# A decoder layer's cross-attention: the chunk of a key piece stands between its transposes and its weighting, not behind the weighting

## The reference

```python
qh = split_heads(layernorm(x) @ Wq)      # 8 heads of 128
kh = split_heads(context @ Wk)
vh = split_heads(context @ Wv)
sim = einsum('hid,hjd->hij', qh, kh) * 128 ** -0.5
mean = mean(sim, axis=-1, keepdims=True)
sim = (sim - mean) * 1.5 + mean
attn = softmax(sim, axis=-1)
out = einsum('hij,hjd->hid', attn, vh)   # heads side by side, then
x = x + out @ Wout + bout
```

## Time and profile before

| | us |
| --- | --- |
| median of 3 runs (2559.46 to 2560.4) | 2560.4 |
| profiled execution, its own time | 2556.83 |
| its span, first to last instruction | 2555.0 |
| PE busy | 2504.5 |
| DVE busy | 1912.5 |
| ACT busy | 1611.2 |
| granted clock of TensorE, mean over the span | 0.999 |

### The profile page before, as it was taken

The page is one execution under the profiler, slowest core; times in us unless marked ns, Lnnn a source line. Parts: engine busy times, 40 slices in busy tenths (PEclk is TensorE's granted clock), DMA queues, the critical chain, the costliest instruction groups (busy, mean ns, idle before and its releaser), DMA issues. The chain is left out here.

```text
span 2555.0 us, 47085 instructions
## 1 busy us (share of the span) xinstructions
PE 2504.5 (98%) x17639; PEld 2284.5 (89%) x17639; DVE 1912.5 (75%) x3606; ACT 1611.2 (63%) x3049; POOL 157.9 (6%) x208
## 2 busy tenths in 40 slices
PE   7999989999999999999999999999999999999998
PEld 6899868999999999989999899999999999999987
DVE  5899777777777777768777777777777777777787
ACT  6899646565656566565666566656655666655666
POOL 1344220000000000000000000000000000000013
PEclk9999999999999999999999999999999999999999
DMA  7655441002100210012000300031002100110001
GB/s 218 194 160 148 149 174 33 17 17 90 43 24 19 79 54 18 16 67 75 17 17 21 112 18 17 17 108 34 17 17 83 50 17 17 66 69 18 29 1 34
DMA packets 61326, 151.68 MB, mean 59 GB/s; under 512 B 11456, under 2 KB 25024, under 8 KB 61152
## 3 DMA queue, kind: packets, MB, share of 16 engines
q1 hardware_dynamic: 55504, 136.02, 16.4%
q0 software_dynamic: 3248, 12.72, 1.5%
q10 hardware_dynamic: 2400, 0.59, 0.1%
HBM read 126.10 MB, written 23.20 MB: 58 GB/s over the span
## 5 line engine op out<-in xcount | busy, mean ns | idle before, releaser
L1733 PE MATMUL xo_ps<-pt_hi,values 128*128 128x256 f32 x4096 | 950.3, 298 | 2.4 <-DVE pt_lo L1836 2.3
L1755 ACT CAST pt_hi<-xt_ps 128x512 fp32r<-128x512 f32 x1024 | 593.6, 585 | 550.4 <-PE xt_ps L1722 531.7
L1836 DVE TENSOR_TENSOR pt_lo<-xt_ps,pt_hi 128x512 fp32r<-128x512 f32 x1024 | 704.4, 688 | 235.3 <-ACT pt_hi L1755 230.3
L1824 DVE TENSOR_SCALAR_CACHE_REDUCE xprobs<-xs_ps 128x1024 f32<-128x1024 f32 x512 | 627.0, 1225 | 178.1 <-PE xs_ps L1657 173.2
L1733 PEld LDWEIGHTS xo_ps<-pt_hi,values 128*128 128x128 f32 x4096 | 693.0, 188 | 6.1 <-DVE pt_lo L1836 2.6
L1722 PE MATMUL xt_ps<-ident,xprobs 128*128 128x128 f32 x4096 | 603.4, 272 | 0.0
L1762 ACT ACTIVATE xprobs<-xprobs,xneg_max 128x1024 f32<-128x1024 f32 x512 | 591.4, 1155 | 0.2 <-DVE xneg_max L1831 0.2
L1733 PE MATMUL xo_ps<-pt_lo,values 128*128 128x256 f32 x2048 | 570.1, 278 | 0.0
L1722 PEld LDWEIGHTS xt_ps<-ident,xprobs 128*128 128x128 f32 x4096 | 487.6, 140 | 62.1
L1733 PEld LDWEIGHTS xo_ps<-pt_lo,values 128*128 128x128 f32 x2048 | 388.3, 190 | 2.3
L1657 PE MATMUL xs_ps<-k_hi,q_hi 128*128 128x512 f32 x1024 | 327.3, 400 | 1.2 <-DVE values L1884 0.9
(11 more groups left out here) (235 smaller groups left out, 2510.2 us busy)
## 6 DMA issues: line engine op xcount, KB each, us to landing
v_split<-ctx_split SPq DMA_DIRECT2D x68, 768.0 KB, 5.7
xq<-x_split SPq DMA_DIRECT2D x64, 512.0 KB, 3.3
values<-rel_split SPq DMA_DIRECT2D x32, 256.0 KB, 3.5
ctx_split<-ctx_out POOLq DMA_DIRECT2D x8, 768.0 KB, 4.0
q_split<-attn_late SPq DMA_DIRECT2D x16, 256.0 KB, 2.9
k_split<-attn_late SPq DMA_DIRECT2D x16, 256.0 KB, 3.7
values<-q_split SPq DMA_DIRECT2D x32, 128.0 KB, 3.6
values<-k_split SPq DMA_DIRECT2D x32, 128.0 KB, 3.9
```

Of the source, the lines that this page charges most:

```text
L1733: last = pe.matmul(o_ps[:, 0:GQ], v[:, vs], pt[:, c % 3, GQ * j:GQ * (j + 1)], start=c == 0 and j == 0 and m == 0, stop=c == PIECES - 1 an ...
L1755: act.copy(pt_hi[:, c % 3, :], t_ps[:, c % 3, :]).then_inc(t_rounded, 1)
L1824: dve.tensor_scalar(probs[:, par if kind == "A" else 1 - par, t, CHUNK * i:CHUNK * (i + 1)], s_ps[:, buf, :], LOGIT, None, ALU.mult, ALU.m ...
L1836: dve.tensor_tensor(pt_lo[:, c % 3, :], t_ps[:, c % 3, :], pt_hi[:, c % 3, :].bitcast(F32), ALU.subtract).then_inc(t_ready, 1)
```

## The change

`with_pieces` gets a switch, `weigh_first`. With the switch off, as it is unless it is given, the items of piece c now stand between the transposes of c and the weighting of c-2. With the switch on they stand where they were, behind the weighting. It is on for `STEP_8` and `LAST_8`. Since pieces 0 and 1 have no weighting behind their transposes, nothing moves there. In an ordinary step nine chunks change places with a weighting: those at pieces 2, 4, 6, 7, 8, 10, 12, 14 and 15. DVE's, ACT's and SP's lists stay as they are, since they have no item `"W"`.

```diff
-def with_pieces(extra, ahead=()):
+def with_pieces(extra, ahead=(), weigh_first=False):
 
     items = list(ahead)
     for c in range(PIECES):
         items.append(("T", c))
+        if not weigh_first:
+            items += extra.get(c, [])
         if c >= 2:
             items.append(("W", c - 2))
-        items += extra.get(c, [])
+        if weigh_first:
+            items += extra.get(c, [])
     return items + [("W", PIECES - 2), ("W", PIECES - 1)]
...
 STEP_8 = with_pieces({0: [("K+", 2)], 1: [("I",), ("K+", 3)], 2: [("Q+",), ("out",)], 3: [("V+", 4)], 4: [("A", 0, 0)],
...
-                      14: [("E", 0, 2), ("A", 1, 2)], 15: [("V+", 1), ("E", 0, 3), ("A", 1, 3)]}, [("O",)])
+                      14: [("E", 0, 2), ("A", 1, 2)], 15: [("V+", 1), ("E", 0, 3), ("A", 1, 3)]}, [("O",)], weigh_first=True)
...
-LAST_8 = with_pieces(merged({1: [("I",)], 4: [("out",)]}, MIX_8), [("O",)])
+LAST_8 = with_pieces(merged({1: [("I",)], 4: [("out",)]}, MIX_8), [("O",)], weigh_first=True)
```

## The result

| | before | after |
| --- | --- | --- |
| median, us | 2560.31 (22 runs) | 2564.13 (22 runs) |
| lowest to highest, us | 2557.97 to 2564.03 | 2562.43 to 2565.83 |
| ratio after to before | | 1.0014 (95% interval 1.0008 to 1.002) |
| profiled span, us | 2555.0 | 2561.0 |

The kernel became slower by about 3.8 us, 0.14%. That is within the 0.2% that the prediction called no change, but it is on the other side of its 2559.0 and 0.6 us above its range. With 22 runs on each side the interval excludes no change.

The account below looks back on a forecast made before the run. The prediction took PE, busy for all of every ordinary step, to bound the kernel. Order +3.6 us and head change -5.0 us made -1.4 us, from a median of 2560.4 to 2559.0, range 2550.5 to 2563.5.

Parts of the forecast that it names:

- No idle time to fill, and no new wait: In the steps PE is busy throughout, so moved chunks fill no idle time; no wait for a buffer is added.
- The tightest buffer: At pieces 6, 7, 8 of an ordinary step, the buffer A 1 3 wants is emptied with 1.05 us to spare.
- How fast the weightings run: In changed steps all fast weightings but the last two turn slow, 0.17 us of lost speed per ordinary step.
- The rival by which the speeds stay mixed: In changed steps as many weightings stay fast as now: -4.5 - 5.0 = -9.5 us, 2550.9; chance 0.26.
- The seams: Where chunk and weighting swap behind transposes, 0.01 us is given back; five places make -0.05 us per ordinary step.
- The orders' whole price: Slower weightings and seams over all changed steps: about +0.09 us in each of 40 ordinary steps, others together 0; +3.6 us.
- The head change: At seven head changes loads are released 0.71 us sooner, so K+ 3 waits less: 5.0 us saved.
- The argument that the whole pack moves: At the head change the neighbouring loads' releases move by the same 0.71 us, so the earlier issue lands earlier.
- The sum: Whole kernel: +3.6 - 5.0 = -1.4 us, a median of 2559.0.
- the transfer doesn't come sooner: At the head change the DMA engines are the limit, so +3.6 us alone: 2564.0; chance 0.10.

Follow-up runs that it names:

- e5: Kernel before, with each exponential taking 128 of its 1024 columns; executed once under the profiler, ordinary step 30.79 us, as before.
- e6: Changed kernel, with each exponential taking 128 of its 1024 columns; executed once under the profiler, ordinary step 30.99 us against 30.97.
- e7: Kernel before, with only the chunks at pieces 12 and 14 of ordinary steps put ahead of the weighting; profiled once, step as forecast, 30.84 us.
- e9: Changed kernel, with the load for K+ 3 bringing one of its three parts; 2560.15 us against 2560.15 for the kernel before, ratio 1.0.
- e4: Kernel before, with the load for K+ 3 bringing one of its three parts; 2551.45 us against 2560.58, ratio 0.9963.
- e2: Changed kernel, with the old order put back in STEP_7 alone; 2569.06 us against 2560.58 for the kernel before, ratio 1.0029.
- e1: Kernel before, with the new order in STEP_7 alone; 2556.08 us against 2560.58, ratio 0.998.
- e8: Kernel before, old order, with K+ 1 alone one piece sooner in STEP_7 (piece 12, not 13); 2552.58 us against 2560.15, ratio 0.9969.

## Why the prediction was wrong

**No idle time to fill, and no new wait: right.** PE was busy for the whole of every step after as before, and the list of waits has none for `freed` in the moved chunks. The tightest buffer was never near: `A 1 2` was emptied by 1271.77 and its buffer wanted at 1272.90 in the trace after, 1.13 us to spare, where 1.05 was worked out.

**How fast the weightings run: right.** The forms left have no fast weighting among them, as forecast from counting them; e5 and e6 show that it isn't ACT's work that sets the pace, and e7 that taking the form away from two weightings slows those two. In the ordinary step weightings 7, 9 and 11 lost 0.07 us and weighting 5 with `Q+` 0.05, both as forecast. The rival by which the speeds stay mixed, with its 2550.9, is out.

**The seams: this term was mis-sized.** The prediction let a moved score chunk save 0.01 us for being followed by a weighting, taken from one place, the chunk at piece 15. A moved chunk measured 1.48, not 1.47. The chunk at piece 15 had been shorter in the kernel before because it stood behind a weighting at the fast pace: 1.39 there, 1.40 behind one at 0.118 us a matmul. The chunk at piece 2 of the kernel before tells the two apart. It stands behind a fast weighting too (weighting 0) but is followed by transposes, and it also takes 1261.01 - 1259.62 = 1.39.

```profile
1259.62 0.62 PE L1657 MATMUL xs_ps<-k_hi,q_hi 128*128 128x512 f32 x2
...
1261.01 0.60 PE L1722 MATMUL xt_ps<-ident,xprobs 128*128 128x128 f32 x4
```

So the 0.01 belonged to the fast pace, and went with it. Seven moved score chunks hold some 0.08 us of that error in each ordinary step. In the step the prediction had +0.09 us and measured +0.18; in those like `STEP_1` -0.03 and measured +0.06; in those like `STEP_7` +0.03 and measured +0.12. All three are 0.09 too low, which over 56 steps makes 5.0 us. The orders' whole price, put at +3.6, was +8.7 by e9 against e4, and +8.8 in the steps of the two profiles.

The prediction also misread what the seam is. It took the 0.08 us for a weight load that isn't hidden behind transposes. Its own rows show no such thing. The last of the four transposes and the second matmul of the weighting behind them:

```profile
1268.73 0.27 PE L1722 MATMUL xt_ps<-ident,xprobs 128*128 128x128 f32 x1
...
1268.96 0.28 PE L1733 MATMUL xo_ps<-pt_lo,values 128*128 128x256 f32 x1
```

The load for the weighting starts with the last transpose, at 1268.73, and the next load 0.11 later, at 1268.84, as if the weighting's first matmul started there. Only the first matmul's start is put down early, 0.03 us behind the last transpose, and the second follows 0.20 later. Together that is 0.23, what a transpose (0.109) and a matmul of the weighting (0.113 to 0.118) take elsewhere. So four transposes cost PE 4 x 0.109 = 0.43 us wherever they stand, 0.08 of it read as part of the item behind them, and no order of the items has a seam to win. With the seam's term at nothing, the prediction's count gives +0.17 us in an ordinary step (its lost speed alone), about +0.05 in those like `STEP_1` and +0.11 in those like `STEP_7`, against the measured 0.18, 0.06 and 0.12: about +8 in all.

**The head change: right.** The release moved by exactly the 0.71 us: from the end of `K+ 1` to where `K+ 3` could start was 7.55 us before and is 8.26 after. This pair of profiles gave back 4.2 us of the 5.0, but the load's own time from issue to landing scatters from trace to trace. In the four traces that release it as before (before, e2, e5, e7) the seven waits sum to 7.3, 9.0, 9.6 and 8.8 us, in the three that release it 0.71 sooner and whose load is whole (after, e1, e6) to 2.9, 4.3 and 3.8. The means, 8.7 and 3.7, differ by 5.0. The timed runs say the same: the order costs 8.7 (e9 against e4) and the whole change 3.8, which leaves 4.9 for the head change. The argument that the whole pack moves fits this change, but e8 shows that the loads needn't move together.

**The sum.** The order cost 8.7 us and the head change gave back 4.9, by timed runs; the prediction had +3.6 and -5.0. The sign turned on the seams' 5.0 us. The measured time equals the rival "the transfer doesn't come sooner" to 0.1 us, but that is luck: the transfer did come sooner, and two errors of that rival's sum, 5 us each, cancelled.

What stays open: what the fast pace of PE is, and why a load of the same size takes 6.2 to 7.5 us when issued 3.5 us behind another and 7.4 to 8.4 when issued 4.6 behind it.

## What to carry to other kernels

When PE is busy for the whole of a step, an order of its items is worth only what the pace of the items is worth, and each hundredth of a microsecond counts as often as the loop turns: here 0.18 us, 40 times. Take such a term from places that differ in one thing only, not from one place that differs in two. A cost that stands behind every block of one kind, whatever follows, belongs to the block, and moving items can't win it. A wait for a load is cheaper to take away by moving the one item that releases the load (e8, 7.6 us faster) than by a rule for every item of every step.

## What the runs showed of the hardware that was not expected

- PE runs the same weightings at two paces, 0.113 and 0.118 us a matmul of 128x256 with its weight load. The pattern repeats in every turn of the loop, stays as it is when ACT's work falls by 5.5 us a step (e5), and depends on what ran in the step before (e7).
- Behind four 128x128 transposes the next item is put down as starting 0.03 us after the last of them and looks 0.08 us longer than elsewhere: a score chunk 1.48 and not 1.40, a weighting 0.79 and not 0.71. The transposes look as much shorter: 0.36 and not 0.43.
- Two pairs of context blocks issued 3.5 us apart kept the DMA engines busy for 0.97 of the time at 375 GB/s until the second had landed. Issued 4.6 us apart they were busy for 0.81 at 294 GB/s, and the second landed 1.2 us later against its issue, in the mean of seven heads.
